# A two-layer decoder on one core: ternary and convolution weights made ahead of the experts, the scaling of passing tokens spread over the rounds, GpSimd's fade and gather first

## The reference

```python
# layer 0: self attention with relative positions, cross attention, then
x = layernorm(x + L0_ffn(x))      # experts: 7 of 128 slots each, top 2 of 8; expert 8 passes tokens on
#   h = relu(inputs @ experts_inter[e]);  out = (h @ experts_out[e]) * in_w
#   combined[used] += out;  combined += x * (noop_w * noop_mask)
# layer 1
x = layernorm(x + L1_attn(x))     # gated linear recurrence: M = M*decay + (g*k) v,  y = q M; a norm inside too
x = layernorm(x + L1_xattn(x, ctx))
x = layernorm(x + L1_ffn(x))      # below
def weight_quant(w):
    scale = 1.0 / clip(mean(abs(w)), 1e-5)
    return clip(round(w * scale), -1, 1) / scale
h = bit_linear(x, w1)             # activations to 8 bits a token, weights to -1, 0, 1
h = depthwise_conv1d(h, conv_w, conv_b)   # 3 taps along the sequence
out = bit_linear(silu(h), w2)
```

## Time and profile before

| | before |
|---|---|
| median of three runs | 776.01 us |
| the profiled execution, its own time | 766.87 us |
| its span, first to last instruction | 765.1 us |
| mean granted TensorE clock | 0.974 |
| PE busy | 679.4 us (89%) |
| DVE busy | 574.4 us (75%) |
| ACT busy | 406.0 us (53%) |
| POOL busy | 207.2 us (27%) |

### The profile page before, as it was taken

The page is one execution under the profiler, slowest core; times in us unless marked ns, Lnnn a source line. Parts: engine busy times, 40 slices in busy tenths (PEclk is TensorE's granted clock), DMA queues, the critical chain, the costliest instruction groups (busy, mean ns, idle before and its releaser), DMA issues. The chain is left out here.

```text
span 765.1 us, 20966 instructions
## 1 busy us (share of the span) xinstructions
PE 679.4 (89%) x8334; PEld 518.2 (68%) x8334; DVE 574.4 (75%) x1629; ACT 406.0 (53%) x1172; POOL 207.2 (27%) x212
## 2 busy tenths in 40 slices
PE   5778999999999999999887977899899999999886
PEld 2445677777777778777776966666666666666664
DVE  1346787888888999897756676888888887888853
ACT  3665665667766666664310213555555555555542
POOL 4312333333222233423553132222222222222100
PEclk9977899999999999999989999999999999999999
DMA  9766353444555543570032110000000001110000
GB/s 345 276 227 208 129 169 110 143 158 156 169 170 169 170 162 125 173 253 12 26 111 69 32 33 8 9 12 12 12 13 12 16 12 14 14 15 13 5 6 7
DMA packets 48256, 72.20 MB, mean 94 GB/s; under 512 B 2832, under 2 KB 43280, under 8 KB 45472
## 3 DMA queue, kind: packets, MB, share of 16 engines
q1 hardware_dynamic: 45120, 61.80, 24.0%
q0 software_dynamic: 2320, 5.18, 3.1%
q10 hardware_dynamic: 720, 3.88, 1.3%
HBM read 32.38 MB, written 38.47 MB: 93 GB/s over the span
## 5 line engine op out<-in xcount | busy, mean ns | idle before, releaser
L1062 ACT ACTIVATE sc<-sc,nmxa 128x128 f32<-128x128 f32 x256 | 80.9, 390 | 50.0 <-DVE nmxa L1288 49.3
L497 POOL TENSOR_TENSOR early<-early,recb 128x616 f32<-128x616 f32 x32 | 38.8, 1215 | 194.4 <-DVE recb L1374 194.4
L1656 DVE TENSOR_TENSOR k<-bank,k_sb 128x512 f32<-128x512 f32 x64 | 41.1, 685 | 29.9 <-PE bank L556 29.9
L1284 DVE TENSOR_TENSOR sc<-bank,rel 128x512 f32<-128x512 f32 x64 | 41.1, 683 | 14.0 <-PE bank L556 8.4
L1296 DVE COPY pTa<-bank 128x512 f32<-128x512 f32 x32 | 22.0, 689 | 34.9 <-PE bank L617 34.9
L1042 ACT ACTIVATE rext<-bank 128x512 f32<-128x512 f32 x64 | 34.8, 610 | 20.9 <-PE bank L556 20.9
L533 POOL TENSOR_TENSOR oTb<-x_all,row_sb 128x128 f32<-128x128 f32 x16 | 7.6, 475 | 141.1 <-DVE pTa L1677 133.6
L556 PE MATMUL bank<-k,xdT 128*128 128x512 f32 x96 | 45.5, 610 | 0.0
L474 POOL TENSOR_TENSOR rext<-rext,ones 128x1008 f32<-128x1008 f32 x16 | 29.9, 1867 | 56.1 <-ACT rext L1042 56.0
L1109 ACT ACTIVATE early<-early 128x308 f32<-128x308 f32 x64 | 28.2, 453 | 30.7 <-DVE early L1359 30.5
L617 PE MATMUL bank<-k_sb,sc 128*128 128x128 f32 x256 | 37.4, 294 | 7.3 <-issue 6.5
(11 more groups left out here) (274 smaller groups left out, 1851.4 us busy)
## 6 DMA issues: line engine op xcount, KB each, us to landing
rel_dram<-rext SPq DMA_DIRECT2D x16, 2040.0 KB, 7.3
rel<-rel_dram SPq DMA_DIRECT2D x16, 960.0 KB, 5.5
rext<-w_up SPq DMA_DIRECT2D x1, 1792.0 KB, 10.1
rel<-w_down SPq DMA_DIRECT2D x1, 1792.0 KB, 8.3
wb<-w_b ACTq DMA_DIRECT2D x1, 1604.0 KB, 17.0
xT_ld<-xT SPq DMA_DIRECT2D x16, 64.0 KB, 7.3
x_all<-x ACTq DMA_DIRECT2D x1, 1024.0 KB, 12.1
rel<-rel_dram SPq DMA_DIRECT2D x16, 64.0 KB, 5.6
```

The source lines that it names most:

```text
L497: G.tensor_tensor(pB[:, part, :], pB[:, part, :], recb[:, part].unsqueeze(2).broadcast_to([P, 8, C]), ALU.mult).then_inc(b_even, 1)
L1062: last = A.activation(sc[:, h, :], sc[:, h, :], ACT.Exp, bias=nmxa[:, h:h + 1])
L1284: added = mark(V.tensor_tensor(sc[:, part[i], :], bank[2 * j + i][:].rearrange("p (a j) -> p a j", a=4), rel[:, t % 2, part[i], :], ALU.add))
L1656: V.tensor_tensor(scd[:, 4 * i:4 * i + 4, :], bank[(1, 2, 0, 1)[i]][:].rearrange("p (a t) -> p a t", a=4), const("causal").unsqueeze(1).br ...
```

## The change

Six edits:

- PE: the product that sums the weights' sizes is put ahead of the transposes of the gathered slots.
- DVE: `mean_sizes` and both `ternary` stand ahead of `m_turn`, and are gone from the expert loop.
- POOL: the multiplication of the taps stands ahead of `gather(0)`. `d_fade(0)` and `gather(1)` are written by hand behind it, so that `d_res(0)` comes after them.
- ACT: `d_sig(0)` is written by hand behind `d_gates(0)`; DVE: `d_gate(0)` is written by hand behind the loop.
- DVE: the three `pass_by` between the loop and the table are gone; `c_s0(t)` does `pass_by(t + 2)` at t = 2, 6 and 10.
- `BEGUN2` says so.

```diff
-BEGUN2 = dict.fromkeys(("gather", "c_s0", "c_s1", "c_st", "c_ag", "c_ln", "c_norm", "d_x", "d_qk", "d_gv", "d_gates", "d_r0",
-                        "d_r1", "d_rope", "d_rank"), 1)
+BEGUN2 = {**dict.fromkeys(("c_s0", "c_s1", "c_st", "c_ag", "c_ln", "c_norm", "d_x", "d_qk", "d_gv", "d_gates", "d_gate",
+                           "d_sig", "d_fade", "d_r0", "d_r1", "d_rope", "d_rank"), 1), "gather": 2}
...
-            gather(0)
             pool.wait_ge(ld_conv, 32)
             pool.wait_ge(w_ready, 2)
             G.tensor_tensor(wconv, wconv, fw[:, 0:HID].unsqueeze(1).broadcast_to([P, 3, HID]), ALU.mult
                             ).then_inc(w_ready, 1)
+            gather(0)
+            d_fade(0)
+            gather(1)
...
             idle(3, 15)
+            pe.wait_ge(w_sum, 1)
+            mm(bank[7][:, 0:2], ones[:], wabs[:]).then_inc(w_mean, 1)
             for n in range(2 * E):
...
-            pe.wait_ge(w_sum, 1)
-            mm(bank[7][:, 0:2], ones[:], wabs[:]).then_inc(w_mean, 1)
...
             d_gates(0)
+            d_sig(0)
             run(ORDER2["act"], {
...
             def c_s0(t):
+
+                if t % 4 == 2 and t + 2 < B:
+                    pass_by(t + 2)
                 dve.wait_ge(ld_g[t % 3], 32 * (t // 3 + 1))
...
+            mean_sizes()
+            for i in range(2):
+                ternary(i)
             m_turn(1)
             m_turn(3)
-            mean_sizes()
             m_hid(1)
...
-                if n < 5:
-                    ternary(n // 2)
...
-            for t in (4, 8, 12):
-                pass_by(t)
-
+            d_gate_(0)
             run(ORDER2["dve"], {
```

## The result

| | before | after |
|---|---|---|
| median, 20 runs each on one chip | 774.63 us (769.59 to 778.54) | 769.77 us (761.91 to 773.35) |
| the profiled execution, its own time | 766.87 us | 767.5 us |
| its span | 765.1 us | 765.7 us |
| mean granted TensorE clock | 0.974 | 0.972 |
| PE, DVE, ACT, POOL busy | 679.4, 574.4, 406.0, 207.2 us | 679.3, 571.0, 406.4, 206.8 us |

The ratio is 0.9942 [0.9924, 0.996]: faster by 4.5 us, 4.9 by the medians. The forecast was 773.8, so 2.2 faster, with a range that ended at 771.4. Note that the two profiled executions alone would have said "0.6 us slower".

What follows compares the result with a forecast made beforehand. DVE was taken to bound the kernel from 435 us to layer 1's first scores. -3.6 + 1.4 = -2.2 us gave 764.7 us for the profiled execution and 773.8 us for the median, range 771.4 to 776.6.

Steps and rivals of the forecast that it cites:

- What bounds the kernel: From 435 us to layer 1's first scores DVE sets the end, through a long cast and three scalings.
- The three waits of PE: PE waiting for DVE before `m_down(11)`, `d_x(0)` and `d_s01(0)`: 1.74, 0.92 and 0.91 us.
- The weights block hidden: Product, means and ternaries ahead of the experts fit DVE's idle time with 0.5 us to spare: cost 0.
- Term 1: Start of layer 1: first scores `d_s01(0)` come 3.6 us earlier, then bounded by PE's dummies.
- Term 2: Spread scalings in the steady rounds: hidden at t = 2, 0.72 us each at t = 6 and 10, +1.4 us.
- A (the gather late): Start of layer 1: first gather lands 1.7 us later, total 775.5 us; chance 0.20.
- B (the clock doesn't fall): The PE clock fall at 470 to 473 us stays out, 1.5 us more won, 772.3 us; chance 0.21.
- C (each scaling drops the clock): Rounds 2, 6 and 10 cost 2.2 us each through clock falls, total 779.1 us; chance 0.06.
- the change doesn't reach the end: Rival: POOL's and DVE's part is won but the steady rounds absorb it; chance below 5%.
- I see no part of that in the changed stretch, so I carry the difference as it is: Final sum: the median's 9.1 us above the profiled execution is added unchanged, giving 773.8 us.

Runs made afterwards that it cites:

- s2: The changed kernel, unchanged, run again on another chip beside the kernel before: 764.61 us, ratio 0.9985.
- s3: The kernel before with only the early weights block and the taps ahead of the first gather; scalings, gate and fade as before: 762.71 us, ratio 0.9958.
- s6: The changed kernel, unchanged, measured a third time, on the second follow-up chip: 765.93 us, ratio 0.998 to before.
- s8: The changed kernel, unchanged, measured a fourth time, on the third follow-up chip: 763.99 us, ratio 0.9963 to before.
- s7: The changed kernel with scalings moved into DVE's wait behind the keys' product, plus seven dummy products in PE's early waits: 762.17 us, ratio 0.9946 to before.
- s11: Like s7, but five instead of eight dummy products in front of the first scores: 760.41 us, ratio 0.9901 to before.

## Why the prediction was wrong, and where it was right

**What bounds the kernel: right.** The three waits of PE and their two causes were the right ones. The weights alone removed two of them, and the third stayed until the scalings left.

**The weights block hidden: right, with less to spare.** In s2, whose trace has no stall here, the block ended at 414.41 and DVE then waited 0.20 us for the slots; the forecast left 0.5. In the trace of after the copies came directly behind the block and still PE's down products did not wait. The copies did not wait for POOL, although both stand beside the multiplication of the taps. DVE in s2, where POOL multiplies the taps from 414.56 to 418.00:

```profile
414.61 0.69 DVE L1571 COPY pTb<-bank 128x512 f32<-128x512 f32 x1 [0.20 <-PE bank L829]
415.65 0.42 DVE L1571 COPY pTb<-bank 128x256 f32<-128x256 f32 x1 [0.35 <-PE bank L829]
```

The first took 0.69 us in the kernel before as well, with POOL idle.

The Trainium skill, "SBUF — State Buffer", "Who interferes with whom", says that a VectorE instruction with at most one input in SBUF doesn't contend with GpSimd outside its two-port modes, but that casts and copies in such a mode lock GpSimd out or wait for it in full. These copies read PSUM and ran freely; the cast, which reads and writes SBUF, took 3.86 us beside the taps and takes 0.41 alone. Both agree. Who was first the rows can't settle: by their starts the cast was, 0.14 us ahead of the multiplication, and still it was the one that waited. The prediction also priced a full wait of 0.45 us wherever a scaling meets one of POOL's sums. In after none met, by the rounds of 18.72. Where three scalings and two sums do meet (s3), DVE lost 0.28 us in all, less than one sum, and POOL 0.75, about one scaling; whether POOL waited in full for one of them stays open.

**Term 1: right.** Forecast -3.6, measured -3.60 in the shown pair and -3.8 in the pair of one chip; over all traces of the two kernels without a clock fall in the experts it is 39.35 to 39.92 us against 43.45 and 43.52, so -3.5 to -4.2. The gather is what `c_s0(0)` waits for next (0.91 us), and the dummies are what the scores wait for.

**Term 2: right for the two on the chain, too low by 0.34 at t = 2.** Forecast 2 x 0.72 and nothing at t = 2. Measured 18.72 against 18.00 twice, 1.4 us more from `c_s0(4)` to the end, and 1.45 us back when the scalings went into a wait; at t = 2 the idle time was taken up, but 0.34 came on top in the round from `c_s0(3)` to `c_s0(4)`.

**The rivals.** A (the gather late): from the start of its second half to `c_s0(0)` are 2.96 us in after, 0.4 more than the 2.6 of the earlier trace rows, not 1.7. B (the clock doesn't fall): at 470 to 473 us it stood at 1.00 after, where the earlier trace rows has 0.50, but it fell earlier:

```profile
458.00:461.00 3.00, 1.37 (x13) 0.82 (x5) 1.56 (x8) 1.35 (x6) 0.00 (x0) 0.86 0.00 0
461.00:464.00 3.00, 3.00 (x16) 2.87 (x16) 2.09 (x7) 0.86 (x4) 0.87 (x2) 0.58 0.00 0
```

The clock given up here is (0.14 + 0.42) x 3 = 1.7 us; in s6 it was 1.7 as well, in s2 and s8 3.4. The size of the fall comes and goes with the same code, so it is no effect of the change. C (each scaling drops the clock): refuted, since rounds 6 and 10 were longer by 0.72 and no more. The last one (the change doesn't reach the end): refuted, since from `c_s0(4)` on all rounds but 6 and 10 kept their 18.0 us, and the shift with them.

**The step that failed** is the last: "I see no part of that in the changed stretch, so I carry the difference as it is". It took the 9.1 us between the median of the runs shown and the profiled execution for a constant of both kernels. The miss is 773.8 - 769.77 = 4.0 us. Of it, 776.01 - 774.63 = 1.4 us is before itself, which ran faster than its three first runs said; 4.9 - 2.2 = 2.7 us is the larger difference between the kernels. The excess of before was no constant: on three other chips it ran at 766.40, 767.53 and 766.58, where the profiled execution lies. There the change was worth 1.3, 2.2 and 2.9 us, on average 2.1 ± 0.5, which is the forecast's 2.2; in the measurement of the result it was 4.9 ± 0.8, which is 2.8 ± 1.0 more. In the measurement of the result both kernels were slower than elsewhere, before by 7 to 8 us and after by 4 to 6, and the gain seen there contains this unlike excess. The range was too narrow in the same way: it allowed 1 us for runs, where twenty runs of one kernel covered 11 us.

**What stays open** is what the excess is. A lower clock isn't enough: the mean of the changed kernel was 0.970 there and 0.971 to 0.973 elsewhere, and from run to run 0.001 of clock goes with some 0.6 us, so 0.4 to 1.3 us of the 4 to 6. Executions with the same clock say it directly: at 0.973 the changed kernel took 767.54 and 768.58 us there, and 762.71 to 764.68 in eight executions on the other chips. The one trace from that measurement has the two stalls of 3.69 and 5.94 us that the profile puts down to "remote", and none of the other twelve traces (before's and the eleven here) has any such wait. They are of the right size (5.71 us later at the last scatter than in s2), they lie outside the changed code, and how many an execution meets would be chance. But the execution that has them took 767.5 us, 2.3 less than the median of its own measurement; there is no trace of before from that measurement; and on the other three chips no trace shows them. Nor can I exclude that the change gains 2 us more in such a disturbed execution than in a quiet one. That the result differs from the three repetitions is shown; that the stalls are the reason is only argued.

## What to carry to other kernels

Put the profiled execution beside the median before you add anything to it: if they lie 1% apart, the median holds time that no row explains, and that part belongs into the range and not as a constant into the sum. An instruction that is much longer than its like, with no wait shown in front of it, may be waiting inside for another engine; find what ran beside it and move one of the two, before you look at its own cost. And when a wait in front of deliberate filler work (here the dummies) is removed, the filler becomes the bound: cut it in the same step, which won 1.2 us at the first scores here, where the spreading of the scalings won 0.9 and gave 1.4 or more back. Price each edit by itself for the same reason: the weights alone did at least as well as the whole change (1.9 ± 0.7 us better on one chip, level on another).

## What the runs showed of the hardware

- A 32x512 cast from f32 to bf16 in SBUF took 3.86 us beside a 128x1536 multiplication on POOL and 0.41 without it; a copy of 128x512 out of PSUM took 0.69 us beside the same multiplication and without it. Three 128x512 products with both inputs in SBUF took 2.41 us beside POOL's two sums and 2.13 alone, the sums 1.68 us instead of 0.93.
- The granted clock falls by different amounts in the same code: 1.7, 3.4, 1.7 and 3.4 us of clock were lost between 450 and 474 us in four executions of the changed kernel, whose first two rounds took 29.82, 31.97, 29.99 and 32.20 us. With seven dummy products in PE's waits there (two executions, s7 and s11) it stayed at 1.00.
- Twenty executions of one kernel on one chip covered 761.91 to 773.35 us.
